# A two-layer language-model tower on one core: tokens as rows, weights in three groups, gathers first, and a convolution tap on ScalarE

## The reference, cut

```python
x = embed_matrix[tokens]                              # tokens (4, 1024), table (50257, 192)
# layer 0, mixer; `normed` is layernorm(x)
xc, z = split(normed @ W_in, 2)                       # (4, 1024, 192) each
xc = silu(depthwise_conv3_causal(xc, conv_w) + conv_b)
y = cumsum(xc, axis=1) * sum(B * C, -1) + xc * D
x = x + (y * silu(z)) @ W_out
# layer 0, second block: router scores, attention for the 15% lowest-scored tokens,
# a mixing path for the others, GELU feed-forward
# layer 1: attention over tokens and over 100 memory slots, gated fusion,
# then a feed-forward with ternary weights and 8-bit activations
wq = clip(round(w / mean(|w|)), -1, 1) * mean(|w|)    # for w1 and w2
```

## Time and profile before

| | us |
|---|---|
| median of 3 runs | 1915.02 |
| fastest, slowest | 1910.84, 1923.53 |
| profiled execution | 1911.3 |
| its span, first to last instruction | 1909.6 |
| PE, DVE, ACT, POOL busy | 1615.0, 1296.8, 978.4, 127.7 |

### The profile page before, as it was taken

The page is one execution under the profiler, slowest core; times in us unless marked ns, Lnnn a source line. Parts: engine busy times, 40 slices in busy tenths (PEclk is TensorE's granted clock), DMA queues, the critical chain, the costliest instruction groups (busy, mean ns, idle before and its releaser), DMA issues.

```text
span 1909.6 us, 26407 instructions
## 1 busy us (share of the span) xinstructions
PE 1615.0 (85%) x9798; PEld 902.6 (47%) x9798; DVE 1296.8 (68%) x3017; ACT 978.4 (51%) x1393; POOL 127.7 (7%) x165
## 2 busy tenths in 40 slices
PE   0759887988999999996557898889899999999835
PEld 0357646564333333355334584656523333333814
DVE  4666674026899998946778487531489889996478
ACT  0422353214777777762732325431357777777345
POOL 6010000000000000002420100000000000000020
PEclk9977898999899999998678687989989999999957
DMA  6003220007101000000110212000430010000001
GB/s 155 1 1 116 54 62 1 1 1 210 38 30 30 26 26 26 17 1 5 30 34 0 83 51 77 21 1 1 131 109 26 26 34 26 26 26 1 1 1 34
DMA packets 53894, 73.39 MB, mean 38 GB/s; under 512 B 18712, under 2 KB 27205, under 8 KB 53767
## 3 DMA queue, kind: packets, MB, share of 16 engines
q1 hardware_dynamic: 52150, 68.54, 12.4%
q0 software_dynamic: 1616, 3.16, 0.7%
HBM read 38.51 MB, written 33.17 MB: 38 GB/s over the span
## 4 chain that ended last, share of the span: by engine, by line
PE 68%; DVE 22%; ACT 4%; issue 2%; DMA 2%; POOL 1%; SPq 1%; DVEq 0%; ACTq 0%
PE PV L906 10%; PE ST L890 9%; PE S L856 7%; PE ST L802 4%; PE ST L557 4%; PE MT L856 3%; PE PV L915 2%; DVE nmp L1545 2%; DVE st L1418 2%; PE S L813 2%; DVE amax L1653 2%; DVE R L1652 2%; PE ST L587 1%; PE S L851 1%; DVE Er L1473 1%
## 5 line engine op out<-in xcount | busy, mean ns | idle before, releaser
L1234 ACT ACTIVATE Er<-ST 128x1024 f32<-128x1024 f32 x384 | 377.1, 1021 | 105.6 <-PE ST L890 105.3
L1597 DVE TENSOR_REDUCE nmp<-S 128x1 f32<-128x512 f32 x514 | 337.4, 683 | 30.6 <-PE S L856 30.6
L890 PE MATMUL ST<-QS,KS 100*128 100x512 bf16 x768 | 218.0, 385 | 0.3
L906 PE MATMUL PV<-Er,V 128*17 128x512 f32 x1536 | 211.6, 600 | 0.0
L856 PE MATMUL S<-KS,QS 96*128 96x512 bf16 x514 | 183.4, 392 | 0.9
L1597 DVE TENSOR_REDUCE nmp<-MT 128x1 f32<-128x512 f32 x254 | 173.4, 683 | 13.5 <-PE MT L856 13.5
L856 PEld LDWEIGHTS S<-KS,QS 96*128 96x128 bf16 x514 | 48.3, 98 | 154.8 <-DVE nmp L1597 103.7
L451 POOL TENSOR_SCALAR tp<-mv 128x8 f32<-128x8 f32 x20 | 5.6, 278 | 1667.2 <-DVE mv L1422 1667.2
L1545 DVE TENSOR_REDUCE nmp<-S 128x1 f32<-128x512 f32 x120 | 77.4, 683 | 48.5 <-PE S L672 48.2
L890 PEld LDWEIGHTS ST<-QS,KS 100*128 100x128 bf16 x768 | 72.1, 99 | 64.3 <-ACT Er L1234 5.7
L856 PE MATMUL MT<-KS,QS 96*128 96x512 bf16 x254 | 99.4, 391 | 0.9 <-DVE nmp L1597 0.9
(11 more groups left out here) (387 smaller groups left out, 3079.7 us busy)
## 6 DMA issues: line engine op xcount, KB each, us to landing
KS<-scr_k SPq DMA_DIRECT2D x72, 192.0 KB, 2.7
scr_k<-R SPq DMA_DIRECT2D x16, 576.0 KB, 4.0
QS<-scr_q SPq DMA_DIRECT2D x48, 192.0 KB, 2.8
scr_k<-R SPq DMA_DIRECT2D x16, 384.0 KB, 4.6
QS<-scr_k SPq DMA_DIRECT2D x24, 192.0 KB, 2.5
scr_q<-R SPq DMA_DIRECT2D x8, 576.0 KB, 4.7
scr_k<-R SPq DMA_DIRECT2D x16, 192.0 KB, 5.2
scr_q<-R SPq DMA_DIRECT2D x8, 384.0 KB, 5.0
```

The lines of the kernel that those rows point to most:

```text
L890: ins = nc.tensor.matmul(ST[i % 2][:, (kt % 2) * HALF:(kt % 2 + 1) * HALF], KS[0:KP + 4, k, kt * P:(kt + 1) * P], QS[0:KP + 4, k, half * H ...
L906: ins = nc.tensor.matmul(PV[row:row + VC, :], slots[h // H].V[:, kt, h % H, :], E[:, step % RING, (kt % 2) * HALF:(kt % 2 + 1) * HALF], st ...
L1234: A_(E[:, g, :], ST[i % 2][:, :], ACT.Exp).then_inc(s["exps"], 1)
L1597: v.tensor_reduce(nmp[:, u // 2, u % 2:u % 2 + 1], bank, AX.X, ALU.max).then_inc(s["reduced"], 1)
```

## The change

Loads get three semaphores. `early`: memory features, `wmem`, its bias, `w1`, `w2`, issued first. `loaded`: `win`, `convw`, `cols`, `bmat`, `cmat`. `rest`: all others. `wmem` moves to its own room in Er, `w1` and `w2` to HS of slots a and z. The tokens are loaded by SP as 32 rows of 128 numbers; DVE copies them to f32, PE transposes them, DVE copies them back to integers in `tok_i`. POOL makes only the identity and `neghalf` first, then gathers slot a and five tiles of z, the deviation of a, three tiles of z, the deviation of z, and after that the other constants. Some fills move from POOL to DVE. In pair 0 DVE's list is written out anew; the late fills stand between two convolutions. PE and ACT turn, evacuate and project slot a before slot z for c = 0, in both pairs. The ternary weights are turned after the projections. ACT does the convolution's last tap with its bias (`Identity`, from PSUM into `Y1[c]`), and the product with D (into `DY`, in X); `Y1[1]` lies in HS.

```diff
-                sp.dma_start(dst, src, allow_slow_non_contiguous=True).then_inc(s["loaded"], 16)
-                n[0] += 1
...
+            sp.dma_start(tok_r, A["x"].rearrange("b (t p) -> (b t) p", p=P)).then_inc(s["tokens"], 16)
+            load(memn, A["L1_attn_memory_features"][0], "early")
+            load(wmem[0:CH, :, 0:2 * D], cm(A["L1_attn_w_mem"]), "early")
...
+            load(w1, cm(A["L1_ffn_w1"], P), "early")
+            load(w2, cm(A["L1_ffn_w2"]), "early")
+            load(win[:], cm(A["L0_attn_W_in"]), "loaded")
...
 @block.gpsimd
-            g.wait_ge(s["tokens"], 16)
-            for o in slots:
-                gather(0, o)
+            g.wait_ge(s["tokens"], 18)
+            gather(0, a)
+            gather(0, z, range(0, 5))
+            inverse_deviation(0, a, 0)
+            gather(0, z, range(5, T))
+            inverse_deviation(0, z, 0)
+            late_consts()
 @block.tensor
-            pe.wait_ge(s["consts"], NCONST)
-            pe.wait_ge(s["filled"], 3)
-            pe.wait_ge(s["loaded"], LOADED)
+            pe.wait_ge(s["consts"], 1)
+            pe.wait_ge(s["tokens"], 17)
+            nc.tensor.transpose(ST[1][:, 0:NB * T], tok_f, ident[0:NB * T, 0:NB * T]).then_inc(s["pp"], 1)
+            pe.wait_ge(s["filled"], 1)
+            pe.wait_ge(s["early"], EARLY)
...
-                for o in slots:
-                    turn_norm(p, o, 0)
-                for c in range(2):
-                    for o in slots:
-                        inproj(p, o, c)
+                turn_norm(p, a, 0)
+                if p == 0:
+                    pe.wait_ge(s["loaded"], LOADED)
+                inproj(p, a, 0)
+                turn_norm(p, z, 0)
+                inproj(p, z, 0)
+                for o in slots:
+                    inproj(p, o, 1)
+                if p == 0:
+                    turn_ternary()
+                    pe.wait_ge(s["wprep"], 4)
+                    pe.wait_ge(s["rest"], OTHERS)
+                    pe.wait_ge(s["consts"], NCONST)
+                    pe.wait_ge(s["filled"], 3)
+                    pe.wait_ge(s["pa"], 5)
 @block.scalar
                     if i < 2:
-                        A_(o.XC[...], o.R2[n % 2][0:CH, :], ACT.Copy).then_inc(o.s["inproj_out"], 1)
+                        if n == 4:
+                            act.wait_ge(o.s["stored"], p * 32 + 32)
+                            act.wait_ge(s["pd"], 5)
+                        A_(o.XC[...], o.R2[n % 2][0:CH, :], ACT.Copy)
+                        A_(o.Y1[c][...], o.R2[n % 2][0:CH, :], ACT.Identity, scale=convw[:, c, 2:3], bias=cols[:, c, 0:1]).then_inc(o.s["inproj_out"], 1)
...
-                A_(o.Y1, o.Y1, ACT.Silu).then_inc(o.s["silu"], 1)
+                A_(o.Y1[c], o.Y1[c], ACT.Silu).then_inc(o.s["silu"], 1)
+                act.wait_ge(o.s["silu"], p * 2 + c + 1)
+                if c == 1:
+                    act.wait_ge(o.s["gated"], p * 2 + 1)
+                A_(o.DY, o.Y1[c], ACT.Copy, scale=cols[:, c, 1:2]).then_inc(o.s["dterm"], 1)
...
+                evac(p, a, 0, a.XT)
+                inproj(p, a, 0)
+                evac(p, z, 0, z.XT)
+                inproj(p, z, 0)
+                for o in slots:
+                    conv(p, o, 0)
+                for o in slots:
+                    inproj(p, o, 1)
+                for o in slots:
+                    conv(p, o, 1)
+                if p == 0:
+                    ternary()
 @block.vector
+            def late_fills():
+                link(v.memset(ksm[KP:KP + 4, :, :], 1.0))
+                v.memset(ksm[KP:KP + 2, :, :], 0.0).then_inc(s["filled"], 1)
+                for o in slots:
+                    v.memset(o.XT[CH:CH + 1, 1, :], 1.0).then_inc(s["pa"], 1)
+                ve.wait_ge(s["loaded"], LOADED)
+                link(v.tensor_tensor(bmat[:], bmat[:], cmat[:], ALU.mult))
+                link(v.tensor_reduce(cols[:, :, 6], bmat[:], AX.X, ALU.add))
...
-                link(v.tensor_scalar(o.Y1, o.XC[:, c, 2:L + 2], convw[:, c, 2:3], cols[:, c, 0:1], ALU.mult, ALU.add))
...
-                link(v.tensor_scalar(o.Y1, o.Y1, cols[:, c, 1:2], None, ALU.mult))
+                ve.wait_ge(o.s["dterm"], p * 2 + c + 1)
...
+                if p == 0:
+                    ve.wait_ge(a.s["gathered"], 128)
+                    stats(p, a, a.U)
+                    split_memory()
+                    ternary(w1, w1q[:, 0:FC, :], P, 0)
+                    normalise(p, a, 0, a.U, a.rn)
+                    ternary(w2, w2q[0:CH, :, :], CH, 1)
+                    ve.wait_ge(z.s["gathered"], 128)
+                    stats(p, z, z.U)
+                    normalise(p, z, 0, z.U, z.rn)
...
                     for o in slots:
                         convolve(p, o, c)
+                        if p == 0 and c == 0 and o is a:
+                            late_fills()
```

More of the change, by code:

```diff
@@ L248, in build @@
         splm = Er[0:CH, 2048:2048 + 3 * MSP].bitcast(BF16).rearrange("p (a c n) -> p a c n", a=3, c=2)
[L249 to L253, removed]
+        wmem = Er[0:CH + 1, 2720:2720 + 4 * D].rearrange("p (c n) -> p c n", c=2)
+        w1 = slots[0].HS[:, 0:FC, :]
+        w2 = slots[1].HS[0:CH, :, :].rearrange("p t d -> p (t d)").rearrange("p (t f) -> p t f", t=2)
+        tok_r = Er[0:NB * T, 3488:3488 + P].bitcast(I32)
+        tok_f = Er[0:NB * T, 3616:3616 + P]
+        names = """early rest wprep qones loaded consts tokens outproj h1 logit expz score srow_turned srow_copied picks rank_turned rank_copied premixed precopied pt gathersel nts
             units0 reduced0 units reduced rowmax mturned mcopied acc0 ctxr accout st0 ex0 pv0 ctxn ctxt ctxtc att atts
@@ L283, in build @@
         QR = ("qr0", "qr1", "qr2", "qr3")
-        loads = []
+        loads = {"early": 0, "loaded": 0, "rest": 0}
         a, z = slots
@@ L405, in _ @@
                 sp.wait_ge(o.s["stored"], NPAIR * 32 + 32)
-        LOADED = loads[0] * 16
-        NCONST = 14
+        EARLY, LOADED, OTHERS = loads["early"], loads["loaded"], loads["rest"]
+        NCONST = 9
         @block.gpsimd
@@ L431, in _, with late_consts @@
             const(g.tensor_copy(identb[:], ident[:]))
[L432 to L444, removed]
-            for o in slots:
-                const(g.memset(o.NTS[CH:CH + 1, :, :], 1.0))
-                link(g.memset(o.QS0[KP:KP + 4, :, :], 0.0))
-                const(g.memset(o.cnt[:], 0.0))
+            link(g.memset(neghalf[:], -0.5))
+            def late_consts():
+                link(g.memset(earlier[:], 1.0))
+                const(g.affine_select(out=earlier[:], in_=earlier[:], compare_op=ALU.is_gt, fill=0.0, base=0, pattern=[[-1, P]], channel_multiplier=1))
+                link(g.iota(slot_i, pattern=[[QP, 2], [1, QP]], base=0, channel_multiplier=0))
+                const(g.tensor_copy(slot[:], slot_i))
+                link(g.iota(rowslot_i[:], pattern=[[QC, 2]], base=0, channel_multiplier=1))
+                const(g.tensor_copy(rowslot[:], rowslot_i[:]))
+                const(g.memset(acc_mem[:], 0.0))
+                for o in slots:
+                    const(g.memset(o.NTS[CH:CH + 1, :, :], 1.0))
+                    link(g.memset(o.QS0[KP:KP + 4, :, :], 0.0))
+                    const(g.memset(o.cnt[:], 0.0))
             def rsqrt(o, dst, src, eps, h=slice(0, T)):
@@ L465, in inverse_deviation, with gather @@
                 g.tensor_tensor(o.rnn[:], o.rnn[:], o.rn[:], ALU.mult).then_inc(o.s["rstd"], 1)
-            def gather(p, o):
-                for t in range(T):
+            def gather(p, o, tiles=range(T)):
+                for t in tiles:
                     b = 2 * p + o.x
@@ L482, in _ @@
                 g.wait_ge(s["qones"], p + 1)
-                for n in range(5):
+                for n in range(0 if p else 1, 5):
                     for o in slots:
@@ L1376, in _ @@
             v.memset(rec[:, 6:8], 0.0).then_inc(s["pv0"], RING0)
+            link(v.memset(vm[:], 0.0))
+            v.memset(vm[:, :, DH:DH + 1], 1.0)
+            v.memset(memt[CH:CH + 1, :, :], 1.0)
+            v.memset(splm[:, :, :, :], 0.0)
+            v.memset(ones[:], 1.0)
+            v.memset(PV[:, :], 0.0)
+            v.memset(MTf, 0.0)
+            v.memset(rec[:, 8:10], 0.0).then_inc(s["filled"], 1)
+            ve.wait_ge(s["tokens"], 16)
+            v.tensor_copy(tok_f, tok_r).then_inc(s["tokens"], 1)
+            ve.wait_ge(s["pp"], 1)
+            v.tensor_copy(tok_i[:], ST[1][:, 0:NB * T]).then_inc(s["tokens"], 1)
             for o in slots:
+                v.memset(o.rn[:], 0.0).then_inc(o.s["evac"], 2)
                 v.memset(o.rnn[:], 0.0).then_inc(o.s["stored"], 32)
@@ L1407, in _, with split_memory @@
-            link(v.reciprocal(wscale[:], wsinv[:]))
-            for w, q, n, c in ((w1, w1q[:, 0:FC, :], P, 0), (w2, w2q[0:CH, :, :], CH, 1)):
+            def split_memory():
+                ve.wait_ge(a.s["hi"], 1)
+                kmem = S[1][0:CH, 0:2 * P].rearrange("p (c n) -> p c n", c=2)[:, :, 0:MS]
```

(4 more changed lines are left out.)

141 lines of the change are left out of this document (61 added, 80 removed).

## The result

The changed kernel took **1899.23 us** (median of 4 runs, 1895.01 to 1903.30), the kernel before in the same comparison 1918.66 (1910.84 to 1923.53): ratio 0.9912, 95% interval 0.9884 to 0.9939. It is faster, as forecast, but by 19.4 us where 35 were forecast; 1899.2 lies above the range of 1869 to 1896, and 0.9% falls to the outcome "within 1%", which had a chance of 0.06. The profiled execution took 1903.3 us (span 1901.6, granted clock 0.892, beside 1909.6 and 0.902).

The account below looks back on a forecast made before the run. PE holds 68% of the chain, but at the start and convolution stage no engine is full; they hand over. Pair 0 saves 32.4 us, pair 1 0.7: 1911.3 becomes 1878.2, with the median forecast at 1880, range 1869 to 1896.

Parts of the forecast that it names:

- N: The moment DVE begins to normalise slot a; in pair 0 forecast at 28.2 us, before at 59.89.
- mark: DVE's first addition of the convolution's result; in pair 0 forecast at 79.6 us instead of 112.0.
- the 5.8 us kept for it: Start: if eight gathers beside DVE's fills each took 0.72 longer, 5.8 us later; no slowdown was taken.
- That is covered by 0.6 only; with 6.7 to landing behind the last weights it costs 4.: ACT's first evacuation: keys' write landed at 30.1, data at 30.7, so no cost; a 6.7 landing costs 4 us.
- Rival 1: Start: gathers or keys' write late behind the weights, 6 to 12 us later, 1884 to 1892; chance 0.20.
- I take none: Convolution stage: clock dip at PE's new 2.9 us stand could lose 1.8, +3.6 for both pairs; none counted.
- Rival 2: Convolution stage: dearer coupling, clock dips in both pairs, late fills in the way, +4 to +7 us; chance 0.08.
- The two coupling steps: Convolution stage: a's silu waits behind z's projection on ACT, costing 1.3 in pair 0; later PE stands 2.9 us.
- the tap and the product with D bring nothing: Convolution stage: DVE saves 6.3 us per pair, nearly all lost to the new coupling of PE and ACT.
- from there to the end of pair 0 the same length as before within 3 us: Behind pair 0's first addition of the convolution's result: code and operands unchanged, so length unchanged within 3 us.
- Rival 4: PE-bound rest: less rest at the start lowers PE's granted clock below 0.902; 1% slower gives 1930; chance 0.02.
- The row with 600 to 850 at 1.00: Long attention stage: clock 1.00 after hundreds of us of full work, cited against a general clock loss.

Follow-up runs that it names:

- after_again: The changed kernel unchanged, run and traced once more: 1897.74 us, ratio 0.9912.
- mw_late: The changed kernel with ACT's wait for the memory keys' write moved from before its first evacuation to behind the ternary copies: 1891.15 us, 0.9859.
- gap_mw: The changed kernel with three unused products in PE's gap and ACT's wait for the keys' write moved late: 1879.87 us, 0.9792.
- gap_filled: The changed kernel with three unused products in PE's gap between the context transposes of slots a and z: 1881.43 us, 0.9802.
- after_4: A fourth trace of the changed kernel as it is: end of span 1901.1 us.
- tap_only: The kernel before with only the convolution's last tap and the product with D on ACT, order and start kept: 1914.76 us, 0.9988.
- no_tap: The changed kernel with tap and product with D back on DVE, start and order kept: 1887.55 us, 0.9862; with the gap also filled, 1878.47 us.

## Why the prediction was half right

The four traces of the changed kernel and the three of the old one, as means, lay the difference open (us; forecast, then measured):

| | forecast | changed kernel | before |
|---|---|---|---|
| N, pair 0 | 28.2 | 26.6 | 58.8 |
| N to scan, pair 0 | 24.5 | 30.7 | 22.9 |
| scan to mark, pair 0 | 26.9 | 28.9 | 29.0 |
| N to mark, pair 1 | 50.9 | 54.4 | 51.9 |
| all the rest of the span | 1746.0 | 1754.2 | 1751.8 |

Of the 19 us by which 1899.2 lies above 1880, 6.6 are lost before the mark, 3.5 in pair 1's stage, and 9 in the rest (8.2 by the means of the traces). The 6.6 and 3.5 are the forecast's own mistakes in the stage; of the 9 about 6 come from the ground it stood on: a profiled execution with two fast draws (its rest was 1746.0, the mean of the three traces 1751.8).

**The start: right.** First gather 5.23 (forecast 5.0), statistics of a at 19.42 (20.6), N 25.95 (28.2), z normalised from 37.87 (38.4), gathers 1.25 apart. The tokens' load and hand-overs, the gathers' landings, the order on DVE and POOL all went about as priced. Beside DVE's fills the gathers took 0.94 or 0.95 us after a first one of 1.22: no slowdown, so the 5.8 us kept for it were not needed. The Trainium skill (GPSIMD Engine Reference, Key points) speaks of contention with instructions in a two-port mode or with two SBUF inputs; by the trace these fills did not slow them. One gather, at 24.58, took 1.65 us. Beside it DVE ran tensor_scalars of one SBUF input, 1152 numbers a partition in 0.76 us; the next gather, beside the normalising, took 0.95. Whether those count as a two-port mode no run shows; the cause is open.

**The failing step, first term: "That is covered by 0.6 only; with 6.7 to landing behind the last weights it costs 4."** The text saw this wait, and took the kind end as its value. The keys' write let ACT go at 32.68, 31.44, 32.37 and 33.37 in the four traces, not at 30.1, while PE had filled the first bank by 28.3 to 29.6. The term that was mis-sized is the landing, taken at the 1.9 us of the kernel before: the six writes now took 4.2 to 6.4 us, and ACT was let go 4.0 to 5.0 us after the last of them had been issued. Issuing them took 2.81 to 4.49 us, where 2.8 was the estimate; with 2.81 (after_again) ACT was still held until 31.44. In the kernel before these writes had the queues nearly to themselves (DMA share 0.31 at 40 to 42); now they fall among the `rest` weights (1.09 at 26 to 29). That the traffic is the reason is argued from this, not tried. Rival 1 had this, as 6 to 12 us; it was 3 to 5 by the traces of mw_late (28.06 for a mean of 30.7) and gap_mw (the mark 4.8 earlier). The timing of gap_mw, 1.6 us less than gap_filled, can't confirm it. A cover of 0.6 us on a chain with three estimates in it is no cover, and the likelier value was some 3.

**Second term: PE's clock, "I take none".** The first projection took 9.40 us for 6.9, its first part at half clock, behind PE's idle times of 7.93 and 4.23. That was nowhere in the sum: it is what is left of the excess when the wait is gone (gap_mw: N to scan 26.78 against 24.5, the projection 9.18). The half clock itself is not new. The forecast took the 6.9 from a kernel in which both slots' transposes had come first and had taken it up; by moving a's projection ahead of z's transposes the change moved it in. The profile's clock column hides this: for 64.81 to 68.37 of the kernel before it shows 1.00, where four transposes still took 1.06 us. Before 65.9 that trace has no record of the clock, and the column shows 1.00 where it has none; there the length of known products has to tell. And behind the new stand of 2.65 us the clock was down for 6.8 us in both pairs (in the four traces seven times 6.8 us and once 3.4), 3.4 us lost on the 24 products (13.68 less 10.3), where the text had named 1.8 per pair as the end of an unknown cost and taken none. Scan to mark is 29.3 against 26.9, and 29.5 against 26.4. Rival 2 described this well and had 0.08. The two coupling steps otherwise came as told: in pair 1, where no keys are waited for, N to scan was 24.6 against 24.5 (in after_4 26.5), and PE's stand 2.65 against 2.9.

**Right: the tap and the product with D bring nothing.** tap_only is 0.9988, and with the gap filled no_tap is worth 3.0 us, within what can be told.

**Wrong for its reason: "from there to the end of pair 0 the same length as before within 3 us".** From the mark to where pair 1 is normalised took 884.5 us in the profiled execution, 874.1 in that of before, and 870.1 in after_again. The code was the same, its time was not: a stage whose clock is drawn anew at a gap has two lengths, 6 to 9 us apart from gap to GELU, and the stretch ahead of it varied by 8 more. Rival 4 expected a general lowering of the clock by less rest; the traces do not show one (the rest of the span has 1754.2 for 1751.8). The row with 600 to 850 at 1.00, which stood against rival 4, spoke for that stretch and for no other. Its evidence for, 0.90 in pair 0 and 0.83 in pair 1, was misread too: pair 0's figure leaves out the half clock until 65.9. With that counted from PE's first transposes at 61.21 it is 0.86, and the two pairs are nearly alike.

Not tried apart: tokens as rows against the order of the loads.

## What to carry to other kernels

Before forecasting from one trace, look for stages where the granted clock is low behind a gap of 2 to 3 us on PE, and take a second trace: such a stage may have two lengths, and the difference can be as large as the change that is judged. To compare two versions, take that draw out of both first, by closing the gap, and expect that others stay: the stage ahead of it still varied by 8 us. Count such a stage from the gap and not from a later event: 6.4 of the 17.0 us lay ahead of the window in which the loss was first seen. When work is moved so that PE comes out of longer idle, or stands for the first time in a row of products (2.65 us was enough here, 1.05 was not), price the products behind at half clock, and never count a cover that is smaller than the error of the chain it rests on.

## What the hardware showed unexpectedly

A gap of 2.36 us on PE was followed, in 14 of 24 cases, by 34 to 38 us at 1.2 GHz, some 25 of them without a break in the matmuls (eight in 2.77 us for 1.46); in the others by 3.4 us, or by none at first. Three unused products in the gap removed this in 12 of 12 stretches and gained 16.3 and 10.7 us. More unused products in two other gaps made the timed kernel 10 us slower.
